# A graph attention layer on one core: scores of the upper triangle only, the lower triangle through DRAM

## The reference

```python
    def _L3_gnn_ref(x, adj, weight, bias, node_w, edge_w):
        node_att = jax.nn.softmax(x @ node_w, axis=0)
        h = x @ edge_w
        e = h @ h.T
        e = jnp.where(adj > 0, e, NEG_BIG)
        edge_att = jax.nn.softmax(e, axis=1)
        combined_att = node_att * edge_att
        support = x @ weight
        output = adj * combined_att @ support
        return output + bias
```

## Time and profile before

| | |
|---|---|
| median of 3 runs | 3040.88 us (3040.13 to 3040.99) |
| the profiled execution | 3041.71 us |
| its span, first to last instruction | 3039.9 us |
| `attention3`, from its first matmul to the end | 2340.78 to 3039.9 us |

### The profile page before, as it was taken

One profiled execution on the slowest core, in us unless ns is written; L12 is line 12 of the kernel. 1 busy time (PEld: TensorE's weight loads), 2 busy tenths in 40 slices (PEclk: granted clock), 3 DMA queues, 4 the chain that ended last, 5 costly groups with the idle time before them and its releaser, 6 DMA issues. The chain is left out here.

```text
span 3039.9 us, 56761 instructions
## 1 busy us (share of the span) xinstructions
PE 2698.9 (89%) x21599; PEld 1649.0 (54%) x21599; DVE 1927.0 (63%) x3518; ACT 1701.3 (56%) x2966; POOL 151.3 (5%) x93
## 2 busy tenths in 40 slices
PE   7929999999993779999999957699499999999999
PEld 4514444444441468888888833344276455555554
DVE  4638999999976688889988764322464333333332
ACT  2328888888872577888888857311233333333322
POOL 3720000000000000000000000000000000000000
PEclk9969999999996889999999979899799999999999
DMA  3033343434323261111111160123432121111210
GB/s 119 0 128 120 129 149 119 161 134 147 110 80 119 83 233 37 39 34 36 30 35 35 27 231 35 52 87 94 164 111 75 53 73 56 61 68 55 74 52 18
DMA packets 129682, 263.03 MB, mean 87 GB/s; under 512 B 58987, under 2 KB 61767, under 8 KB 122331
## 3 DMA queue, kind: packets, MB, share of 16 engines
q1 hardware_dynamic: 123163, 228.89, 22.3%
q10 hardware_dynamic: 6336, 31.72, 3.2%
HBM read 204.44 MB, written 56.14 MB: 86 GB/s over the span
## 5 line engine op out<-in xcount | busy, mean ns | idle before, releaser
L1395 PE MATMUL m_acc<-m_y,m_b 128*128 128x260 f16 x3872 | 662.8, 276 | 51.3 <-DVE m_b L1222 35.3
L1398 PE MATMUL m_acc<-m_y,m_at 128*128 128x130 f16 x3872 | 660.3, 222 | 0.0
L1191 ACT ACTIVATE m_above<-m_u,m_nvs 128x512 bf16<-128x512 f32 (+1 forms) x864 | 521.6, 682 | 93.4 <-DVE m_b L1222 92.3
L1395 PEld LDWEIGHTS m_acc<-m_y,m_b 128*128 128x128 f16 x3872 | 376.7, 97 | 115.8 <-issue 34.9
L804 PE MATMUL m_acc<-keep_z_hi,m_p_hi 128*128 128x512 f16 x968 | 365.6, 378 | 57.3 <-DVE m_p_lo L659 54.3
L1398 PEld LDWEIGHTS m_acc<-m_y,m_at 128*128 128x128 f16 x3872 | 381.3, 98 | 0.0
L805 PE MATMUL m_acc<-keep_z_lo,m_p_hi 128*128 128x512 f16 x968 | 366.0, 378 | 0.0
L808 PE MATMUL m_acc<-keep_z_hi,m_p_lo 128*128 128x512 f16 x968 | 365.1, 377 | 0.0
L1222 DVE TENSOR_TENSOR m_b<-m_above,m_at 128x1024 f16<-128x1024 bf16 (+1 forms) x432 | 278.1, 652 | 69.9 <-PE m_acc L1398 38.5
L2120 DVE CUSTOM_DVE_ANT_0 m_em<-m_sc,m_am 128x512 f32<-128x512 f32 x132 | 85.2, 647 | 327.4 <-PE m_sc L2064 314.5
L2194 ACT ACTIVATE m_wT_hi<-m_tw 128x1024 f16<-128x1024 f16 (+1 forms) x66 | 62.8, 952 | 397.6 <-PE m_tw L2077 397.6
(11 more groups left out here) (268 smaller groups left out, 5382.7 us busy)
## 6 DMA issues: line engine op xcount, KB each, us to landing
m_a_rows<-adj ACTq DMA_DIRECT2D x44, 704.0 KB, 4.6
m_at<-adjT SPq DMA_DIRECT2D x22, 1408.0 KB, 8.3
m_a<-adj SPq DMA_DIRECT2D x22, 1408.0 KB, 6.4
at<-m_at SPq DMA_DIRECT2D x22, 704.0 KB, 4.1
keep_at_first<-at SPq DMA_DIRECT2D x22, 704.0 KB, 4.5
m_at<-at SPq DMA_DIRECT2D x5, 2816.0 KB, 19.5
m_u<-rows SPq DMA_DIRECT2D x40, 256.0 KB, 3.9
p_x_all<-x SPq DMA_DIRECT2D x6, 1536.0 KB, 14.5
```

The source lines that it names most:

```text
L1191: act.activation(pair(above, a % RA, nb)[:, i], u[:, g % RU, 0:nb], ACT.Relu, bias=nvs[:, k, 2 * p + i:2 * p + i + 1], scale=STEEP).then_i ...
L1395: pe.matmul(full.rearrange("p l y e -> p (l y e)"), pair(b01, (m // 2) % RB, nb)[:, m % 2, q // 2, half], y12[:, k % 2, j].rearrange("p l ...
L1398: last = pe.matmul(full[:, :, 1, :], at[:, i0 + q // 2, j, half], y2[:, k % 2, j], start=False, stop=(j == T - 1), skip_group_check=True)
```

## The change

Only `attention3` is changed. Its loops are written out, one tile after the other.

Tile t now computes scores for columns from t * 128 to 2708 only, in chunks of up to 512 (`EC[t]`), 72 chunks in all where there were 132. The columns of those scores that lie two tiles or more to the right of the diagonal are copied by ACT from PSUM to `lw` (`evacuate`) and stored by SP in DRAM, tile by tile, at the row tile j that needs them (`store_low`, runs of 128 float32, 20 in the last column tile). The tile next to the diagonal goes straight from PSUM into `em` of the next row tile. Row tile t fetches its t - 1 stored tiles with one DMA (`load_low`). They are then scores with the column index on the partitions: the transposed layout that `products` wants, so the lower part needs no transposes.

For the lower part the mask comes from `at16` (second half of `mask`), DVE adds it (`add_mask`), reduces over tiles (`lower_max`, a tree of maxima), PE turns the result (`turn_max`), DVE reduces it to one value a row, and `row_max` joins it with the upper part's. The joint maximum is spread again by DVE (`row_copies`) and PE (`spread_max`, after k = 4 of the products), DVE adds it (`subtract`), ACT takes the exponential and the copy (`exp_lower`), DVE the remainder (`low_lower`). The row sum of the lower part is formed by PE, matmuls with one moving column (`sums`), before the products.

The score banks go from 4 to 3 (one bank holds `maxT`, `maxB`, `total`), and a bank is free only after ACT's copy. The residual is added by DVE inside `finish`; POOL has nothing to do beyond two memsets.

The diff, cut to its core:

```diff
+        CW, SB, RL, RX = 512, 3, 3, 3
+        low = nc.dram_tensor("low3", (T, P, (T - 1) * P), F32).ap()
...
+        EC = [[(n0, min(CW, N - n0)) for n0 in range(first(t), N, CW)] for t in range(T)]
+        BASE = [sum(len(EC[i]) for i in range(t)) for t in range(T + 1)]
+        GROUPS = [[(g, min(8, T - g)) for g in range(t, T, 8)] for t in range(T)]
...
+        sc = kit.ps("sc", [SB, CW])
...
+            last = max(len(EC[t + 1]) - 1, 0)
+            return [min(2 * g, last) for g in range(len(GROUPS[t]))]
...
+            steps, n = [], t
+            if n >= 8:
+                steps.append((4, ("em", 0), ("em", 4)))
+                steps += [(min(4, n - k), ("mm", 0), ("em", k)) for k in range(8, n, 4)]
+                n = 4
...
+                    sp.dma_start(a[0:r, first(t):NP], dram["adj"][t * P:t * P + r, first(t):NP]).then_inc(a_in, 16)
...
+                        sp.dma_start(at[:, 0:t, 0:r], dram["at16"][t // 2, :, 0:t, half:half + r]).then_inc(at_in, 16)
...
+                    for slot in range(RL):
+                        sp.wait_ge(l_out[slot], writes(slot, stored_until(t - 2)))
+                    sp.wait_ge(lou_made, t - 1)
+                    if t >= 3:
+                        sp.wait_ge(lol_made, t - 2)
+                    r = rows(t)
+                    src = low[t].rearrange("p (k c) -> p k c", c=P)[:, 0:t - 1, 0:r]
+                    sp.dma_start(em[:, t % 2, 0:t - 1, 0:r], src).then_inc(l_in[t % 2], 16)
...
+                    sp.wait_ge(sc_used, BASE[t] + c + 1)
+                    for j, nj, w in pieces(t, c):
+                        src = lw[:, slot, j * P - n0:j * P - n0 + nj * w].rearrange("p (j c) -> p j c", c=w)
+                        sp.dma_start(low[j:j + nj, :, t * P:t * P + w].rearrange("j p c -> p j c"), src).then_inc(l_out[slot], 16)
...
+                load_mask(2)
+                for t in range(T):
+                    if t + 2 < T:
+                        load_low(t + 2)
+                    if t + 3 < T:
+                        load_mask(t + 3)
+                    for c in range(len(EC[t + 1]) if t + 1 < T else 0):
+                        store_low(t + 1, c)
+                    if t + 1 < T:
+                        load_x(t + 1)
+                    if t > 0:
+                        store(t - 1)
...
+                    n0, n = EC[t][c]
+                    q, r = BASE[t] + c, rows(t)
+                    if q >= SB:
...
+                def sums(t):
+                    pe.wait_ge(hil_made, t)
+                    pe.wait_ge(lol_made, t)
+                    r = rows(t)
+                    for k in range(t):
...
+                def turn_max(t):
+                    pe.wait_ge(tree, TREE[t])
+                    pe.transpose(maxT[0:rows(t), :], mm[:, 0, 0:rows(t)], keep["ident"][:]).then_inc(maxt_made, 1)
+                def spread_max(t):
+                    pe.wait_ge(nmb_made, t)
...
+                    for k in range(T):
+                        if k >= t:
+                            j0s = [j0 for j0, nj in GROUPS[t]]
+                            if k in j0s:
+                                pe.wait_ge(wt_hi, GBASE[t] + j0s.index(k) + 1)
+                                pe.wait_ge(wt_lo, GBASE[t] + j0s.index(k) + 1)
...
+                SPREAD_AT = 4
+                for c in range(len(EC[0])):
+                    chunk(0, c)
+                pe.wait_ge(tail_made, 1)
+                for t in range(T):
+                    if t + 1 < T:
+                        for c in range(len(EC[t + 1])):
+                            chunk(t + 1, c)
+                            for g, at_c in enumerate(after_chunk(t)):
+                                if at_c == c:
+                                    transposes(t, g)
+                    else:
+                        transposes(t, 0)
+                    if t > 0:
+                        sums(t)
+                    if t + 1 < T:
+                        turn_max(t + 1)
+                    products(t)
             @block.vector
...
+                def upper(t, c):
...
+                    q, r, b = BASE[t] + c, rows(t), t % 2
+                    if c == 0:
+                        dve.wait_ge(am_made, t + 1)
+                        if t >= 2:
+                            dve.wait_ge(lou_made, t - 1)
...
+                def add_mask(t):
...
+                    dve.wait_ge(sc_used, BASE[t - 1] + 1)
+                    if t >= 2:
+                        dve.wait_ge(l_in[t % 2], 16 * (t // 2))
+                    dve.tensor_tensor(lower(t), lower(t), am[:, t % 2, 0:t, 0:rows(t)], ALU.add).then_inc(added, 1)
...
+                def lower_max(t):
...
+                    for i, (n, (s0, k0), (s1, k1)) in enumerate(tree_steps(t)):
+                        if i > 0:
+                            dve.wait_ge(tree, TREE[t - 1] + i)
+                        dve.tensor_tensor(mm[:, 0:n, 0:r], of[s0][:, k0:k0 + n, 0:r], of[s1][:, k1:k1 + n, 0:r], ALU.max).then_inc(tree, 1)
...
+                def row_max(t):
...
+                        dve.wait_ge(maxt_made, t)
+                        dve.tensor_reduce(mx[0:r, b, 0:1], maxT[0:r, :], AXX, ALU.max).then_inc(lm_made, 1)
...
+                    dve.tensor_reduce(nm[0:r, b, :], mx[0:r, b, (0 if t > 0 else 1):1 + len(EC[t])], AXX, ALU.max, negate=True).then_inc(nm_made, 1)
...
+                def weight(t):
...
+                    if t > 0:
+                        dve.wait_ge(rsum_made, t)
+                        dve.wait_ge(maxt_made, min(t + 1, T - 1))
...
+                def subtract(t):
...
+                    r = rows(t)
+                    dve.wait_ge(mb_made, t)
+                    dve.wait_ge(tree, TREE[t])
...
+                def low_upper(t):
...
+                    dve.wait_ge(hiu_made, t + 1)
+                    dve.tensor_tensor(w_lo[0:r, n0:N], emf[0:r, b, n0:N], w_hi[0:r, n0:N], ALU.subtract).then_inc(lou_made, 1)
...
+                def low_lower(t):
...
+                    dve.wait_ge(hil_made, t)
+                    dve.tensor_tensor(wT_lo[:, b, 0:t, 0:r], lower(t), wT_hi[:, b, 0:t, 0:r], ALU.subtract).then_inc(lol_made, 1)
...
+                def finish(t):
...
+                    dve.scalar_tensor_tensor(x[0:r, i, :], acc[0:r, b, :], co[0:r, b, :], x[0:r, i, :], ALU.mult, ALU.add).then_inc(part_made, 1)
+                    dve.wait_ge(part_made, t + 1)
+                    dve.tensor_tensor(x[0:r, i, :], x[0:r, i, :], bias[0:r, :], ALU.add).then_inc(fin_made, 1)
...
+                for t in range(T):
+                    if t + 1 < T:
+                        for c in range(len(EC[t + 1])):
+                            upper(t + 1, c)
+                            for g, at_c in enumerate(after_chunk(t)):
+                                if at_c == c:
+                                    move(t, g)
+                            if c == 0 and t > 0:
+                                finish(t - 1)
+                        weight(t)
+                        row_max(t + 1)
+                        row_copies(t + 1)
+                        subtract(t + 1)
+                        low_upper(t + 1)
+                        if t + 2 < T:
+                            add_mask(t + 2)
+                            lower_max(t + 2)
+                        low_lower(t + 1)
+                    else:
...
+                def mask(t):
...
+                        act.wait_ge(at_in, 16 * t)
+                        last = act.activation(am[:, b, 0:t, 0:r], at[:, 0:t, 0:r], ACT.Copy, scale=BIG, bias=-BIG)
+                    last.then_inc(am_made, 1)
...
+                def evacuate(t, c):
...
+                    q = BASE[t] + c
+                    act.wait_ge(tt_made, q + 1)
+                    last = None
+                    if pieces(t, c):
+                        lo, hi = beyond(t, c)
...
+                            act.wait_ge(l_out[slot], before)
+                        last = act.activation(lw[:, slot, 0:hi - lo], sc[:, q % SB, lo - n0:hi - n0], ACT.Copy)
+                    if c == 0 and t + 1 < T:
+                        r = rows(t + 1)
+                        if t >= 1:
+                            act.wait_ge(lou_made, t)
+                            if t >= 2:
+                                act.wait_ge(lol_made, t - 1)
+                        last = act.activation(em[:, (t + 1) % 2, t, 0:r], sc[:, q % SB, P:P + r], ACT.Copy)
+                    if last is not None:
+                        last.then_inc(sc_used, 1)
...
+                def exp_lower(t):
+                    r, b = rows(t), t % 2
+                    act.wait_ge(sub_made, t)
+                    act.activation(lower(t), lower(t), ACT.Exp).then_inc(expl_made, 1)
+                    act.wait_ge(expl_made, t)
+                    if t >= 2:
+                        act.wait_ge(acc_made, t - 1)
+                    act.activation(wT_hi[:, b, 0:t, 0:r], lower(t), ACT.Copy).then_inc(hil_made, 1)
...
+                for t in range(T):
```

(77 more changed lines are left out.)

319 lines of the change are left out of this document (183 added, 136 removed).

## The result

The changed kernel takes 2877.38 us (median, 2876.63 to 2878.14) where the kernel before takes 3040.93: the ratio is 0.9463, with a 95% interval of 0.9446 to 0.9479. The forecast was 2876, the range 2862 to 2908. The profiled execution took 2878.06 us with a span of 2876.3; the forecast for it was 2876.6 with a span of 2874.8. So the sum came out 1.5 us short, and the two terms in it that were off by 3 and 4.5 us have opposite signs.

A forecast was written before the change was run, and what follows sets the result against it. PE's own work bounds the stage: 2369.2 - 2.6 + 497 + 2.4 + 1 + 3 + 0.4 = 2870.4 us, then 0.3 and a 4.1 tail give span 2874.8, median 2876. Range 2862 to 2908.

The forecast's parts named there:

- What bounds the stage: `attention3`: a step is the sum of PE's own work, 30.96 us from tile to tile, so work taken off PE shortens it.
- PE, term by term: PE over 22 steps: scores 139.3, transposes 28.1, products 313.2, `sums` 12, float32 transposes 4.6; together 497 us against 667 before.
- a second stall: Start of `attention3`: 1 us added to the sum for a second stall of PE.
- Crossings at the float32 transposes: PE at `turn_max` and `spread_max`: about 0.15 us a step, 0 to 0.6 possible, 3 us in the sum.
- The start: From first mask to first transposes of `attention3`: transposes at 2369.2 instead of 2366.52, 2.7 us lost.
- The chain: Once-a-step round from `low_lower(t)` to `low_lower(t + 1)`: 17.6 us against PE's 17.2 at t = 18, 0.4 late.
- the bounds, half and 1.3 times: DVE's lower-part passes, taken at 1.10 ns a column: half if bf16 mask is faster, 1.3 times if PSUM and broadcast operands slow one.
- The load of the lower part: `load_low(20)`, 1.2 MB: lands after 6.4 us, needed 8.1 us after its buffer's release; hidden with 1.7 us to spare.
- The waits for `lw`: ACT's `evacuate` of chunk 3 waits some 5 us for a slot; counted at nothing, 18 us kept for range; rival 2894, chance 0.1.
- The clock: PE's granted clock: 2.4 us lost after the stall, 1.00 after 2384; a rival with half clock in late steps gave 2967, chance 0.05.
- the first rival: Chain or low load late from t = 13: 8 us; with DVE passes 1.3 times, 20 to 30, 2895 to 2905; chance 0.2.
- The tail: From `finish` to the end: 4.1 us instead of 4.7, POOL's addition of 1.3 becoming one on DVE of 0.7.

The follow-up runs named there:

- the experiment on the score columns: Changed kernel with PE also computing the left part of each tile's scores, which nobody reads: 3026.78 us, ratio 0.9955.
- the two last edits: On the changed kernel with mask(1) moved: three chunks ahead of tile 0's transposes, mask 2 and load 3 later, 2868.32 us; then six `lw` slots, 2866.33 us.
- spread at 10: Changed kernel with the joint maximum spread after k = 10 of the products instead of k = 4: 2899.83 us, ratio 0.954.
- the late load: Changed kernel with SP's load of the low tiles issued behind the load of the next mask: 2895.87 us, ratio 0.9525.

## Why the prediction was right, and where it wasn't

**What bounds the stage: right.** "A step is the sum of PE's own work" held before and after; 470.85 of 471.00 us, and 149.4 us for 149 in the experiment on the score columns.

**PE, term by term: right.** From the first transposes (2373.67) to the start of `finish` (2872.23) are 498.6 us. The prediction had 497 - 2.6 + 2.4 + 1 = 497.8 for PE and its clock, and 0.3 to `finish`. The scores and `sums` have been tested one by one; the clock behind the stall cost 0.20 x 10.33 = 2.1 us where 2.4 was written. The 1 us for a second stall had no stall to pay for (behind the first transposes PE is busy for 10.33 of 10.33 us); it happens to stand in for 0.8 that `turn_max` took more and 0.3 of the chain. The float32 transposes can be read off the timeline of PE in step 18 from start to start:

```profile
2808.69 0.31 PE L2190 MATMUL m_misc<-keep_ident,m_mm 128*128 128x128 f32 x1
2808.84 0.38 PE L2208 MATMUL m_acc<-keep_s_hi,m_wT_hi 128*128 128x512 f16 x1
...
2811.86 0.38 PE L2210 MATMUL m_acc<-keep_s_hi,m_wT_lo 128*128 128x512 f16 x1
2812.07 0.27 PE L2195 MATMUL m_misc<-keep_ident,m_nmb 128*128 128x128 f32 x1
2812.18 0.38 PE L2208 MATMUL m_acc<-keep_s_hi,m_wT_hi 128*128 128x512 f16 x1
```

`turn_max` takes 0.15 us and `spread_max` 0.11, where 0.11 was written for both: 21 x 0.04 = 0.8 us in all.

**Crossings at the float32 transposes: wrong, 3 us against nearly none.** The step that failed is "about 0.15 a step" for them. In the same fence `spread_max` starts 0.21 us after the matmul ahead of it and the next one 0.11 after that: PE goes straight through. It has 15 matmuls of the products queued between `turn_max` and `spread_max` and never stops for the answer. What the crossing costs is on DVE's side:

```profile
2812.38 2.69 DVE L2323 TENSOR_TENSOR m_em<-m_em,m_misc 128x2432 f32<-128x2432 f32 x1 [1.16 <-PE m_misc L2195]
```

It waits 1.16 to 2.09 us before every `subtract`, 37.0 us in all, beside PE.

**The start: wrong, 2.7 us against 7.2 (7.6 from the first score matmul, which came 0.5 earlier).** The first transposes were forecast for 2369.2 and came at 2373.67. The step that failed is "the copy of chunk 1 stands behind `mask(1)` on ACT, 2.55 us": it priced the mask as an instruction whose input is there. In the kernel before it is, but `a` has one buffer now, and its load is part of the price: 5.79 us from issue to landing, less what passed anyway. The first half of that paragraph was within 2.3 us: the mask began at 2347.08 instead of 2349.40, chunk 3 at 2351.10 instead of 2352.8. Then chunk 4 came at 2358.64 instead of 2356.7, its 12 matmuls took twice their time (12 x 0.21 = 2.5 us, not in the sum at all), and the rest of the 4.5 lies there. The edit that moves `mask(1)` gave 5.6 us back, which closes the case. It is a term mis-sized by one missed wait, and it can be read in the changed kernel's code: `load_mask` begins with a wait for `am_made`.

**The chain: the mechanism and the lateness right, two terms off that cancel.** From the first matmul of `sums(t)` to the end of `low_lower(t + 1)` the trace has 15.5, 15.8, 16.2, 16.7 and 15.4 us for t = 15 to 19, where PE's step takes 18.9, 18.0, 17.2, 16.5 and 16.5. For t = 18 the prediction had 17.6 against 17.2, 0.4 late; it is 16.7 against 16.5, and the step before ends with 1.0 to spare. The chain is 0.9 shorter mostly because the tree of tile 20 took 3.6 us where 4.4 was written. The step is 0.7 shorter because the prediction compared with the step that holds the chunk of tile 19 (276 columns), while from `sums(18)` to `sums(19)` PE has that of tile 20 (148 columns) to do. That 0.3 came out for 0.4 is luck:

```profile
2804.25 2.55 DVE L2333 TENSOR_TENSOR m_wT_lo<-m_em,m_wT_hi 128x2304 f16<-128x2304 f32 x1
...
2815.35 2.82 DVE L2270 TENSOR_TENSOR m_em<-m_em,m_am 128x2560 f32<-128x2560 f32 x1
2818.20 0.69 DVE L2284 TENSOR_TENSOR m_mm<-m_em 128x512 f32<-128x512 f32 x1
2818.93 2.15 DVE L2284 TENSOR_TENSOR m_mm<-m_mm,m_em 128x512 f32<-128x512 f32 x3
2821.11 0.75 DVE L2284 TENSOR_TENSOR m_mm<-m_mm 128x256 f32<-128x256 f32 x2
2821.78 2.69 DVE L2333 TENSOR_TENSOR m_wT_lo<-m_em,m_wT_hi 128x2432 f16<-128x2432 f32 x1
```

```profile
2807.79 0.17 PE L2181 MATMUL m_misc<-keep_ones,m_wT_hi 128*128 128x1 f16 x1
```

```profile
2824.13 0.33 PE L2172 MATMUL m_tw<-keep_ident,m_w_lo 128*128 128x128 f16 x3
2824.61 0.16 PE L2181 MATMUL m_misc<-keep_ones,m_wT_hi 128*128 128x1 f16 x1
```

`low_lower(18)` ends at 2806.80 and `sums(18)` starts at 2807.79. `low_lower(19)` ends at 2824.47, and there PE is late: three transposes at 0.056 from 2824.13 would let `sums(19)` start at 2824.30, and it starts at 2824.61. That is the 0.3 us of the prediction's 0.4. The views of busy time show only half of it, the 0.15 by which 470.85 falls short of 471.00, since the modelled ends of the matmuls fill up the rest, and no wait is listed. It was the step named (t = 18), and the only one of the last five. The passes cost the 1.10 ns a column that were taken from `low` (2.82 us for 2560 columns, 2.69 for 2432, with a bf16 mask, a broadcast maximum in PSUM or neither): neither end of the bounds, half and 1.3 times, was near. Had they cost 1.3 times, 3.5 us more go round, and by the two experiments on the place of `spread_max` (1.9 us later lost 5, 3.9 later 22) that alone costs nearly 20 us; this is worked out and was not run. The rival had needed the late load beside it for its 20 to 30.

**The load of the lower part: right.** `load_low(20)` is issued at 2806.89, lands 5.9 us later and is wanted at 2815.35, 2.5 us to spare where 1.7 had been written (SP's timeline, and the issues of 2340 to 2876 us with KB of each and median time to landing):

```profile
2806.89 0.32 SPq L2101 DMA_DIRECT2D m_em<-low  x1
```

```profile
low<-m_lw SPq DMA_DIRECT2D x32, 256.0 KB, 5.4
...
m_em<-low SPq DMA_DIRECT2D x1, 1216.0 KB, 5.9
...
m_at<-at SPq DMA_DIRECT2D x1, 640.0 KB, 4.9
```

The mask of the lower part, in runs of 256 B, lands after 4.9 us for 640 KB, as the row of `m_c` let expect. It is hidden.

**The waits for `lw`: the mechanism right, the place of cover right.** 12 waits, 31.9 us on ACT, and none on PE in the steps: a store lands after 5.4 us, as "some 5 us" said. The 18 us kept for the range were not needed; the cover ends only at the start, where the two last edits found these waits and took them away.

**The clock: right for this kernel, too low in the rivals.** No hole but that of 0.3 us, no loss after 2384. But the prediction priced the rivals on the chain without a clock of their own, and the runs show that holes of 2 to 4 us cost 0.6 to 0.8 of their sum again in clock (spread at 10: 11.8 and 9.9; the late load: 11.7 and 6.8). By those shares the first rival's 20 to 30 us of waits would have been 12 to 25 dearer than its 2895 to 2905: mostly past the end of the range, 2908. This is an estimate from the two runs.

**The tail: right.** `finish` begins 2876.3 - 2872.23 = 4.1 us before the end, as written.

```profile
2872.23 0.74 DVE L2339 SCALAR_TENSOR_TENSOR m_x<-m_acc,m_co,m_x 20x512 f32<-20x512 f32 x1 [13.51 <-PE m_acc L2210]
```

In sum: 4.5 us too few at the start, 3 too many at the crossings, and several terms off by up to 1. The agreement of 1.4 us at the median is better than the terms deserve; each by itself was good to 5.

## What to carry to other kernels

When one engine is busy for the whole stage, price the change by that engine's own instructions, and use the other views only to ask whether each cover still holds: here PE's time from the first transposes to `finish` fell by 170.1 us (668.6 to 498.6), the start gave 7.2 back and the tail took 0.7 off, which makes the 163.6. A load into a single buffer belongs to the price of the instruction that reads it whenever the reader before it has just been moved or has just finished; look in the code for what the issue waits for. And when a chain goes round once a step, write its length and the engine's step side by side for every late step: the difference says which edit is free (0 to 1 us here in the last steps), and past it each microsecond of wait costs up to two.

## What the runs showed of the hardware beyond that

- Holes in PE's work are paid at the clock as well: holes of 0.8 to 2.1 us, one a step, gave a granted clock of 0.98 over 82 us; holes of 1.7 to 4.0 us gave 0.91 over 110. Their length alone doesn't give the loss: in the run with the late load the clock stayed at 1.00 around a hole of 1.60 us, in the one with the spread at 10 a hole of 1.72 was followed by 1.6 us of loss (0.89 over 15), and those of 2.88 and 4.02 by 3.4 each.
- With the one-column matmuls doubled the clock fell once, to 0.83 from 2835 to 2845 us. A row of 76 of them stands there (2835.15 to 2837.05), with PE 0.3 us late ahead of it; in the changed kernel the same lateness ahead of a row of 38 left the clock at 1.00. Around the longest row, 80 from 2853.95 on, it stayed at 1.00. What of them the clock answers to was not tried.
- A store of 256 KB to DRAM in runs of 512 B lands after 5.4 us in the median, one of 128 KB after 5.4 too and one of 192 KB after 2.7, so it is not the size alone; which part is the queue of transfers ahead of it was not measured apart. With every store issued twice those of 256 KB landed after 4.0 and 4.3 us in the steps, earlier and not later than the 5.6 there before. I have no explanation for that which a run shows.
